# A graph network's last three attentions: three handoffs in another order, the last one's score row by one transpose and DRAM, and a shorter end

## The reference

```python
h = maximum(layernorm(x), 0)
x = x + L0(h, adj)              # needs all graphs (batch norm)
# layer 1, called A: additive scores
Wh = h @ W.T ; s = Wh @ a_src ; t = Wh @ a_dst
e = leaky_relu(s[:, :, None] + t[:, None, :]) where adj else -inf
x = x + softmax(e) @ Wh
# layer 2, called B: scores are products of features, scaled by a_0
e = leaky_relu(einsum('bid,bjd,d->bij', h, h, a_0)) where adj == 1
x = x + softmax(e) @ h
# layer 3, called C: as layer 1, with elu at the end
x = x + elu(softmax(leaky_relu(s1[:, :, None] + s2[:, None, :])) @ Wh)
```

## Time and profile before

| what | value |
|---|---|
| median of 3 runs | 1579.3 us (1578.58 to 1580.75) |
| the profiled execution | 1582.55 us, its span 1580.8 us |
| busy over the span | PE 1409.4 us (89%), DVE 1140.9 (72%), ACT 828.4 (52%), POOL 386.2 (24%) |
| granted PE clock, mean | 0.952 of full speed |
| third stage | from about 438 us to 1564.4 us, 19 turns |
| after the last computation of the output | 1564.4 to 1580.8 us |

### The profile page before, as it was taken

The page is one execution under the profiler, slowest core; times in us unless marked ns, Lnnn a source line. Parts: engine busy times, 40 slices in busy tenths (PEclk is TensorE's granted clock), DMA queues, the critical chain, the costliest instruction groups (busy, mean ns, idle before and its releaser), DMA issues. The chain is left out here.

```text
span 1580.8 us, 33117 instructions
## 1 busy us (share of the span) xinstructions
PE 1409.4 (89%) x12740; PEld 1269.6 (80%) x12740; DVE 1140.9 (72%) x3276; ACT 828.4 (52%) x1825; POOL 386.2 (24%) x337
## 2 busy tenths in 40 slices
PE   5799998899846979999999999999999999999674
PEld 5799998555435869989998999899988999899574
DVE  4566664778635578888888888888888888876733
ACT  4677776122224555564655656656557465563320
POOL 6333430000000323303313133132230331312400
PEclk9999999899957989999999999999999999999786
DMA  9989991367811213223143131331322314202101
GB/s 207 228 194 209 211 208 68 134 235 252 283 35 47 81 41 81 59 78 99 35 107 86 50 94 35 101 94 41 97 67 77 89 35 107 61 21 68 41 9 34
DMA packets 109601, 161.98 MB, mean 102 GB/s; under 512 B 9472, under 2 KB 61312, under 8 KB 107392
## 3 DMA queue, kind: packets, MB, share of 16 engines
q1 hardware_dynamic: 85248, 117.86, 25.9%
q0 software_dynamic: 19584, 33.56, 11.6%
q10 hardware_dynamic: 4608, 8.39, 1.5%
HBM read 151.40 MB, written 41.94 MB: 122 GB/s over the span
## 5 line engine op out<-in xcount | busy, mean ns | idle before, releaser
L851 POOL TENSOR_TENSOR wts_B<-wts_B,off 128x1024 f32<-128x1024 f32 (+7 forms) x128 | 180.0, 1431 | 345.8 <-PE ps L1424 345.8
L1441 PE MATMUL ps<-hP_A,wts_A 128*128 128x129 f32 x2048 | 250.1, 277 | 6.1 <-DVE wts_A L922 3.3
L1441 PE MATMUL ps<-hP_C,wts_C 128*128 128x129 f32 x2048 | 244.6, 280 | 11.1 <-DVE wts_C L922 11.1
L1441 PEld LDWEIGHTS ps<-hP_C,wts_C 128*128 128x128 f32 x2048 | 238.7, 195 | 14.7 <-DVE wts_C L922 12.2
L1441 PEld LDWEIGHTS ps<-hP_A,wts_A 128*128 128x128 f32 x2048 | 239.3, 193 | 8.4 <-DVE wts_A L922 5.1
L1441 PE MATMUL ps<-hV,wts_B 128*128 128x129 f32 x2048 | 244.3, 275 | 1.6 <-ACT xC L1238 1.6
L1441 PEld LDWEIGHTS ps<-hV,wts_B 128*128 128x128 f32 x2048 | 237.1, 192 | 1.8 <-ACT xC L1238 1.8
L922 DVE SCALAR_TENSOR_TENSOR wts_C<-row_C,least_C,ring_C 128x1024 f32<-128x1024 f32 x128 | 173.1, 1366 | 2.5 <-ACT row_C L1204 1.5
L922 DVE SCALAR_TENSOR_TENSOR wts_A<-row_A,least_A,ring_A 128x1024 f32<-128x1024 f32 x128 | 160.8, 1274 | 9.3 <-ACT row_A L1204 8.2
L293 ACT ACTIVATE maskT<-ps 128x1024 fp8e4<-128x1024 bf16 x128 | 131.3, 1026 | 57.0 <-PE ps L335 46.1
L347 PE MATMUL ps<-x,adj_b 128*128 128x129 f16 x896 | 120.9, 223 | 18.1 <-ACT whn L276 14.6
(11 more groups left out here) (229 smaller groups left out, 2711.7 us busy)
## 6 DMA issues: line engine op xcount, KB each, us to landing
adj_b<-in_adj POOLq DMA_DIRECT2D x120, 256.0 KB, 9.8
maskT_scratch<-maskT SPq DMA_DIRECT2D x16, 1024.0 KB, 6.8
ring_A<-maskT_scratch SPq DMA_DIRECT2D x64, 256.0 KB, 3.1
off<-maskT_scratch SPq DMA_DIRECT2D x32, 512.0 KB, 6.5
ring_C<-maskT_scratch SPq DMA_DIRECT2D x64, 256.0 KB, 3.3
xa<-in_x SPq DMA_DIRECT2D x16, 512.0 KB, 4.6
whT_scratch<-whT_s ACTq DMA_DIRECT2D x32, 256.0 KB, 6.4
whT_b<-whT_scratch SPq DMA_DIRECT2D x16, 512.0 KB, 4.8
```

Of the source, the lines that this page charges most:

```text
L851: pool.tensor_tensor(w, w, off_fp8[:, k, k * P:N], ALU.mult).then_inc(S["B", "up"], 1)
L1441: last = nc.tensor.matmul(Q_SLOTS[c // 2 % 2][:, c % 2, 0:PW], wts[x][:, j, c * P:c * P + P], src[:, j, :], start=(j == 0), stop=(j == T - 1))
```

## The change

Four things change.

1. **C's row.** `rows("C", ...)` and `row_power("C", ...)` in two halves each are replaced. PE's `row_once` transposes `us` once, 128 x 8 to 8 x 128. ACT's `store_row` takes the exponential of these 8 partitions, waits for itself and issues a DMA of 4 KB to a DRAM scratch of two slots. SP's `load_row` reads it back on all 128 partitions into `row_e["C"]`. `load_row` stands in SP's queue between the first two masks of A and `load_q`. A keeps its old way.
2. **Three handoffs on DVE.** `columns("C")` goes ahead of `leaky(1)`; `columns("A")` and `exponents("A")` go ahead of `shifts("B")` and weight 5 of C; `shares("B", 1)` goes ahead of that weight 5.
3. **The limits.** Those known early are checked on DVE once after turn 8 (`early_limits`), the rest is one reduction in the last turn (`late_limits`), and the verdict's matmul and `decide` stand inside the third stage. The three checks of reciprocals are folded into `rec_top` by a factor.
4. **The end.** `retire_sems` and the block of checks are gone, the three fallback blocks are one, with one jump an engine, and SP waits for the saves behind the jump.

```diff
+                    def load_row(b):
+                        sp.wait_ge(S["C", "s_out"], (b + 1) * 16)
+                        if b > 0:
+                            sp.wait_ge(S["C", "wts"], b * T)
+                        sp.dma_start(row_e["C"][:, :], row_dram[b % 2].rearrange("t p -> (t p)").partition_broadcast(P)) \
+                            .then_inc(S["C", "s_row"], 16)
...
                         if 1 <= i + 1 < B:
                             load_mask("A", i + 1, 0)
                             load_mask("A", i + 1, 1)
+                        if 0 <= i - 2 < B:
+                            load_row(i - 2)
                         if 1 <= i + 2 < B:
                             load_q(i + 2)
...
                     save(B - 1)
-                    for k in range(3):
-                        sp.wait_ge(S["C", "out"][k], len(range(k, B, 3)) * 16)
...
+                    def early_limits():
+                        nc.vector.scalar_tensor_tensor(apart, sq_all[:, :], 1.0 / EDGE_VALUE, deg_all[:, :], ALU.mult, ALU.subtract)
+                        nc.vector.reduce_max(limit[:, 1:2], r_top[:, :], AXX)
+                        nc.vector.reduce_max(limit[:, 2:3], spread[:, :], AXX)
+                        dve.drain()
+                        nc.vector.tensor_reduce(limit[:, 0:1], apart, AXX, ALU.max, apply_absolute_value=True)
+                        nc.vector.tensor_scalar(fine[:, :], limit[:, 1:2], 0.99 * ROW_MAX, None, ALU.is_le)
+                        for value, most in ((limit[:, 0:1], 0.25), (limit[:, 2:3], 1000.0), (bound_B[:, :], B_MAX), (norm_W[:, :], W_MAX)):
+                            dve.drain()
+                            nc.vector.scalar_tensor_tensor(fine[:, :], value, most, fine[:, :], ALU.is_le, ALU.mult)
+                    def late_limits():
+                        dve.drain()
+                        nc.vector.reduce_max(limit[:, 3:4], rec_top[:, :, :].rearrange("p k t -> p (k t)"), AXX)
+                        dve.drain()
+                        nc.vector.scalar_tensor_tensor(fine[:, :], limit[:, 3:4], LEAST_MAX, fine[:, :], ALU.is_le,
+                                                       ALU.mult).then_inc(f_fine, 1)
+                    def decide():
+                        dve.wait_ge(f_sum, 1)
+                        nc.vector.tensor_scalar(redo[0:1, 0:1], ps[0:1, 7, 0:1], P - 0.5, None, ALU.is_lt)
...
+                        if i == B + 2:
+                            late_limits()
                         if post and not GW:
                             elu_positive()
+                        if i == B + 2:
+                            decide()
+                        if CA:
+                            columns("C", i - 2)
                         if GW:
                             leaky(i - 1, 1)
                         if CA:
-                            columns("C", i - 2)
                             exponents("C", i - 2)
...
                         if CA:
                             weights("C", i - 2, 4)
+                        if nextA:
+                            columns("A", i + 1)
+                            exponents("A", i + 1)
                         if AA:
                             shifts("B", i)
-                        if nextA:
-                            columns("A", i + 1)
+                        if GW:
+                            shares("B", i - 1, 1)
                         if CA:
                             weights("C", i - 2, 5)
-                        if GW:
-                            shares("B", i - 1, 1)
-                        if nextA:
-                            exponents("A", i + 1)
...
+                    def store_row(b):
+                        act.wait_ge(S["C", "s_made"], b + 1)
+                        if b > 0:
+                            act.wait_ge(S["C", "s_out"], b * 16)
+                        nc.scalar.activation(row_s, TOPS["C"][0:T, :], ACT.Exp, scale=1.0 - SLOPE).then_inc(S["C", "s_kept"], 1)
+                        act.wait_ge(S["C", "s_kept"], b + 1)
+                        if b > 1:
+                            act.wait_ge(S["C", "s_row"], (b - 1) * 16)
+                        act.dma_start(row_dram[b % 2], row_s).then_inc(S["C", "s_out"], 16)
...
-                        if CA:
-                            row_power("C", i - 2, 0)
-                        if GW:
                             keep_scores(i - 1, 5)
                             keep_scores(i - 1, 6)
                             keep_scores(i - 1, 7)
+                        if CA:
+                            store_row(i - 2)
+                        if GW:
                             for j in range(1, 4):
                                 score_exps(i - 1, j)
-                        if CA:
-                            row_power("C", i - 2, 1)
...
+                    def row_once(b):
+                        take(free_q, 1, S["C", "s_kept"], b + 1)
+                        pe.wait_ge(S["C", "us"], b + 1)
+                        nc.tensor.transpose(TOPS["C"][0:T, :], us["C"][:, :], ident[:, :]).then_inc(S["C", "s_made"], 1)
...
                                 if j == 4:
-                                    rows("C", i - 2, free_q, 0)
-                        if CA and not AA:
-                            rows("C", i - 2, free_q, 1)
+                                    row_once(i - 2)
...
-                            if c == 0 and CA and AA:
-                                rows("C", i - 2, free_q, 1)
...
-        retire_sems()
...
-        with nc.Block() as block:
...
+                    take(free_p, 1, f_sum, 1)
+                    pe.wait_ge(f_fine, 1)
+                    nc.tensor.matmul(ps[0:1, 7, 0:1], fine[:, :], ones[:, 0:1], start=True, stop=True).then_inc(f_sum, 1)
...
         with nc.allow_non_contiguous_dma("column blocks of adj"), nc.Block() as block:
             @block.sync
             def _(sp):
                 with sp.If(sp.value_load(redo[0:1, 0:1]) != 0):
...
+                sp.end_ifs()
+                for k in range(3):
+                    sp.wait_ge(S["C", "out"][k], len(range(k, B, 3)) * 16)
```

More of the change, by code:

```diff
@@ L76, in gnn_stack_kernel @@
         norm_W = sb("norm_W", [P, 1])
+        limit, fine, redo = sb("limit", [P, 4]), sb("fine", [P, 1]), sb("redo", [1, 1], i32)
         ps = ctx.enter_context(nc.psum_tensor("ps", [P, 8, HALF], fp32))
@@ L920, in weights @@
                             dve.wait_ge(S[x, "exp"], b + 1)
[L921 removed]
+                            dve.wait_ge(S[x, "s_row"], 2 * b + 2 if x == "A" else (b + 1) * 16)
                         nc.vector.scalar_tensor_tensor(wts[x][:, j, :], row_e[x][:, :], least[x][:, j:j + 1], ring[x][:, j % MR, :],
@@ new lines, in again1_scalar @@
+        def again1_scalar(act):
+            with act.Fori(0, B) as b:
+                with act.Fori(0, T) as t:
+                    n = b * T + t
+                    act.wait_ge(logits_ready, n + 1)
+                    nc.scalar.activation(pro[:, :], sco[:, :], ACT.Exp, bias=nmax[:, 0:1],
+                                         accum_out=rsum[:, 0:1]).then_inc(exp_ready, 1)
+                    act.wait_ge(wT_made, n + 1)
+                    nc.scalar.copy(proT[:, :, :].rearrange("p t c -> p (t c)"), pair(1)).then_inc(wT_ready, 1)
+                    act.wait_ge(whT_made, n + 1)
+                    nc.scalar.copy(whT[:, :], ps[:, 4, 0:P]).then_inc(whT_ready, 1)
@@ new lines, in again1_tensor @@
+        def again1_tensor(pe):
+            with pe.Fori(0, B) as b:
+                with pe.Fori(0, T) as t:
+                    n = b * T + t
+                    pe.wait_ge(adj_real, n + 1)
+                    for r in range(T):
+                        last = nc.tensor.transpose(pair(0)[:, r * P:r * P + P], tmp[:, r * P:r * P + P], ident[:, :])
+                    last.then_inc(adjT_made, 1)
+                    pe.wait_ge(w_ready, n + 1)
+                    for r in range(T):
+                        last = nc.tensor.transpose(pair(1)[:, r * P:r * P + P], pro[:, r * P:r * P + P], ident[:, :])
+                    last.then_inc(wT_made, 1)
+                    pe.wait_ge(wT_ready, n + 1)
+                    for r in range(T):
+                        last = nc.tensor.matmul(ps[:, 4, 0:P], hg[:, r, :], proT[:, r, :], start=(r == 0), stop=(r == T - 1))
+                    last.then_inc(whT_made, 1)
+                    pe.wait_ge(whT_ready, n + 1)
+                    for o in range(O2):
+                        last = nc.tensor.matmul(ps[:, 5, o * P:o * P + P], k1_sb[:, o * P:o * P + P], whT[:, :],
+                                                start=True, stop=True)
+                    last.then_inc(y_made, 1)
@@ new lines, in again2_scalar, with again2_tensor @@
+        def again2_scalar(act):
+            with act.Fori(0, B) as b:
+                with act.Fori(0, T) as t:
+                    n = b * T + t
+                    act.wait_ge(rk_made, n + 2)
```

(25 more changed lines are left out.)

721 lines of the change are left out of this document (320 added, 401 removed).

## The result

| | before | changed |
|---|---|---|
| median, us | 1578.94 (1577.65 to 1580.75, 4 runs) | 1565.4 (1563.51 to 1568.43, 4 runs) |
| profiled execution, us | 1582.55 | 1566.15 |
| its span, us | 1580.8 | 1564.4 |

The ratio is 0.9915, 95% interval [0.9896, 0.9935]: **13.5 us faster**. Forecast were 1559.0, within 1547 to 1571. The granted clock is 0.954 on the mean (0.952 before).

What follows compares the result with a forecast made beforehand. PE was taken to bound the stage, busy 61.95 of 64.31 us a turn. 15.5 + 0.9 - 1.6 - 2.0 - 3.4 - 0.5 + 11.4 = 20.3 us off the median of 1579.3 gave 1559.0 us, range 1547 to 1571.

Steps and rivals of the forecast that it cites:

- The chain hangs on POOL's power, which doesn't move against DVE.: Columns of A, steady turns: ACT's chain to A's row follows POOL's power, so only 0.35 us of the stall is gained.
- PE leaves this part 0.48 us earlier.: Rows of C, first place: without row_power between ACT's copies, PE finishes the score products 0.48 us earlier each turn.
- The 0.46 for the second group: Rows of C: the second group of four transposes on PE goes entirely, gaining 0.46 us a turn.
- ACT's 0.35: Columns of A: ACT gains its 0.23 us idle and about 0.1 before the exponents, 0.35 us a steady turn.
- Rival (a): ACT's chain doesn't catch PE, so the 1.6 us stall is gained nearly whole: 1545 us, chance 0.12.
- Turns 0 to 2: First turns: shifts stands behind PE's transpose and the exponents in turn 1, costing 1.6 us; turn 2 comes out at 0.
- C's row: Row through DRAM: a trip of 5.1 to 6.6 us, covered by 3.6 us or more, cost 0 in steady turns.
- Turn 16: Cover for C's row is missing: DVE waits 1.6 to 3.1 us for it, priced at a loss of 2.0 us.
- part of that slowing goes: Turn 16: the first two weights, 4.74 us beside POOL's products, get partly faster if POOL runs while DVE stands.
- Turn 17: Cover is missing: transposes to first weight take 5.9 to 7.4 us, before 3.21, a loss of 3.4 us.
- Early limits: Nine small DVE instructions after turn 8, 2.0 us, mostly covered: a loss of 0.5 us, with ends 0 and 2.0.
- The end: After the last save: one barrier, load and long jump in place of three rounds, a gain of 11.4 us.

Runs made afterwards that it cites:

- e4: The changed kernel with the exponents of A moved behind the shifts of B, its columns staying ahead; 1564.69 us, ratio 0.9898.
- e1: The kernel before with only C's row through DRAM added, the old DVE order and old end kept; 1583.23 us, ratio 1.0018.
- e2: The kernel before with only the order of the handoffs on DVE moved; 1574.79 us, ratio 0.9962.
- e3: The kernel before with only the new end and the early and late limits; 1571.61 us, ratio 0.9948.
- e10: e7 with ACT making the first half of A's row ahead of the second half of B's normed tiles; 1543.4 us, ratio 0.9755.
- e7: e4 with C's row made the old way, by transposes and powers, in turns 16 and 17; 1560.67 us, ratio 0.9869.
- e12: e10 with the early limits moved ahead of DVE's last wait in turn 17; 1543.34 us, ratio 0.9771.
- e8: The changed kernel with SP's three waits for the saves put back ahead of the block's end; 1569.9 us, ratio 0.9935.

## Why the forecast was right in sign and range, and 6 us too low

- **"The chain hangs on POOL's power, which doesn't move against DVE."** This is the step that failed. That the stall would turn up as a wait of PE for `row_A` was right (22.8 us for 22.5), and that `shifts` would hold against `exponents` too (e4: 0.04). But what PE saves ahead of the chain counts only if the chain starts that much sooner. From DVE's share of A's third pair to `sf_B` it took 14.23 us before in turn 5 (786.85 to 801.08) and 14.68 after (783.90 to 798.58); nearly all of the 0.45 is one add, 1.09 us and not 0.69 (1.10 in turn 8 above). It is once per turn, 5 us in 12 turns. The add stands beside one of POOL's masks in both kernels, but earlier in it after (timeline, turn 5, before and then after):

```profile
786.22 1.09 POOL L851 TENSOR_TENSOR wts_B<-wts_B,off 128x512 f32<-128x512 f32 x1
787.16 0.69 DVE L952 TENSOR_TENSOR xB<-xB,xA 128x512 f32<-128x512 f32 x1
...
783.67 1.09 POOL L867 TENSOR_TENSOR wts_B<-wts_B,off 128x512 f32<-128x512 f32 x1
784.22 1.09 DVE L968 TENSOR_TENSOR xB<-xB,xA 128x512 f32<-128x512 f32 x1
```

POOL's next mask begins at 787.27 and at 784.73. The add begins 0.11 us ahead of that before and 0.51 after, and ends 0.59 us behind it both times: it waits for the mask under way. The parts say whose doing it is. This stretch is 14.62 us in e1, 14.27 in e2 and 14.26 in e3, so C's row costs it and the handoffs don't.
- **"PE leaves this part 0.48 us earlier."** A term mis-sized: it measured 0.22 (from the first score product to the first product of A, 9.15 before and 8.93 after). With `row_power` gone from between ACT's copies, PE and ACT alternate over two buffers, and each waits for the other. The row alone gives 0.13 of it (e1: 9.02) and the earlier columns of C the rest (e2: 9.05), so that I had put C's columns at nothing was wrong too. The 0.46 for the second group was right (0.44), ACT's 0.35 measured 0.48 (`sf_B` to PE's second group, 5.11 and 4.63), all of it from the handoffs. The sum of the four, 0.22 + 0.44 - 0.45 + 0.48, is the 0.7 of a turn. That the time still lies in the forecast's range is owed to the range's width of 12 us either way, not to these terms.
- **Rival (a)**, the whole stall gained, was rightly not taken: e10 shows what it needed, another order on ACT, and then it comes.
- **Turns 0 to 2**: -1.1 and -0.1 for -1.6 and 0. The mechanism was right (e4). Up to PE's second group of rows in turn 1 (552.65 before, 552.51 after, in an execution that was 2.1 us ahead) it cost more: 1.5 in turn 1, as forecast, and 0.5 in turn 0, for which I had put nothing. Of that 0.85 comes back before the mark of turn 2.
- **C's row**: nothing in steady turns, as forecast. The trip is 4.9 us (1523.39 to 1528.36), just under the 5.1 to 6.6 that I took: 1.2 us until SP issues the read, 3.6 for the read. The Trainium skill ("DMA: Bandwidth & Descriptors", Anatomy of one DMA) came closer, with an estimated 5.2 in all; the split differs, since the write alone took 1.2 where the page has about 2 us for each transfer. The page fits that figure to DMAs issued by GpSimd, and these two are issued by ScalarE and SyncE. (With 5.2 my sum for turn 17 gives 2.7, not the 2.6 that I wrote.)
- **Turn 16**: -1.8 for -2.0. That "part of that slowing goes" beside POOL was wrong: the first two weights took 4.73 us, as the 4.74 before.
- **Turn 17**: -2.9 for -3.4. The trip costs 2.4 of it (transposes to first weight, 5.57 us and 3.21 before). The other 0.5 is TensorE's clock: while DVE's late weights held TensorE back it was granted 0.50 (the 1.2 GHz level, still so at 1539 to 1543), then 0.80 in the window from 1543 to 1547, then 1.00 (2.4 GHz). The 114 products that follow without a wait for weights took 15.76 us, and 14.94 before; the clock rose 1.7 us later within them. That the longer wait delays the rise isn't shown: e7 hasn't got it, and there they still took 15.43.
- **Early limits**: 1.0, not 0.5 (turns 8 and 9 in e10 and e12), between the ends given.
- **The end**: 10.2 for 11.4. One long jump, 3.70 us, as said. Before, only the third of PE's jumps was long (0.37, 0.22 and 3.77 us), and the records of the other engines' jumps have 0.05 to 0.07. The Trainium skill ("Runtime: NRT & Kernel Launch", Instruction fetch mechanics) says that a taken jump waits for a fetch where its target isn't in the fetched window; one long jump over the longer body agrees with that, but no trace here shows the fetch. What I missed is that the barrier and the load take 2.0 us from the save's issue to PE's jump (1558.29 to 1560.3), not 0.6: 0.8 of it passes from the save's issue to the loads, and the load itself takes 1.1 beside the save (e8). The late limits cost 0.06 us and not 0.25.

## What to carry to other kernels

When a wait is removed and PE's total of waiting stays, look in the table of waits for the name that has come in, and follow that one back: here it led to one line moved on ACT, which gave 18 us by the ratios, more than the whole change. Price a saving by whether the chain behind it starts sooner, not by PE's busy time. A piece of work made shorter also shifts what follows against the other engines: here C's row gave 0.57 us a turn on PE and lost 0.4 of it on one add that now met more of POOL's mask. A DMA that replaces work in a loop needs its cover in each turn, the last ones too: where the tail has none, keep the old way there.

## What the runs showed of the hardware

- POOL's power of 128x8 took 1.64 us beside small things of DVE or none. It took 2.54 to 2.63 us wherever a DVE instruction of 1.2 us with two inputs in SBUF had begun 0.17 us before it (374 powers in the 14 profiles, with no exception). Begun 0.14 to 0.16 us behind the power's start, as in turn 3 of each of the 14, the same product changed nothing, and both kept their length (timeline of the changed kernel):

```profile
686.74 1.64 POOL L856 TENSOR_TENSOR rs_C<-rs_C,mhalf 128x8 f32<-128x8 f32 x1 [14.71 <-DVE rs_C L894]
686.90 1.28 DVE L938 SCALAR_TENSOR_TENSOR wts_A<-row_A,least_A,ring_A 128x1024 f32<-128x1024 f32 x1 [0.23 <-issue]
```

The Trainium skill ("SBUF — State Buffer", SBUF: two separate sides) says that such a VectorE instruction and a GpSimd one that reads SBUF shut each other out, and that the one that starts first holds the shared ports for its whole instruction. The 0.9 to 1.0 us of the first case fit that. The second doesn't: the power's record is 1.64 us long, and the product inside it wasn't held back.
- DVE's add of 128x512 took 0.69 to 1.45 us by the place in POOL's mask at which it began, and ended 0.58 to 0.60 us after POOL's next mask had begun, in turns 1 to 15 of the kernel before, of the changed one, of e1 to e4 and of e7.
- After a write of 4 KB to DRAM SP could issue its waiting read 1.2 us later in steady turns and in the tail alike (14 of 16 turns); the read of that line into 128 partitions landed in 3.5 to 5.1 us.
- Loading one register from SBUF took 0.46 to 0.55 us, the second and third time 0.27 to 0.31 (before), and 1.07 to 1.27 us while a save of 512 KB was in flight (the changed kernel and e3; e8 shows it by taking the save away).
- The granted clock can fall at different places in a sparse stretch of the same program: 6 us earlier in e12 than in e10, with the same instructions there, which cost 1.8 us.
